# Attention on one Trainium2 core: rings of three single PSUM banks for the two kinds of score tiles

## The reference

```python
B, S, E, H = (8, 256, 256, 16)          # run with x of 8 x 512 x 256, so s = 512
q = split_heads(x @ Wq); k = split_heads(x @ Wk); v = split_heads(x @ Wv)
attn = softmax(einsum('bhqd,bhkd->bhqk', q, k) * e ** (-0.5))
attn = attn + bias[None]                # relative bias, added after the softmax
out = einsum('bhqk,bhkd->bhqd', attn, v)
out = (out - mu) / sqrt(var + EPS) * gamma + beta
x = layernorm(x + out)                  # then: router logits of the next layer = x @ router_w
```

## Time and profile before

| | us |
|---|---|
| runs of the kernel before | 1999.19, 1995.83, 1998.24 (median 1998.24) |
| the profiled execution | 1997.37 |
| its span, first to last instruction | 1995.7 |
| TensorE busy, of the span | 1659.3 |
| VectorE busy | 1182.0 |
| ACT busy | 1081.9 |
| GpSimd busy | 614.4 |
| mean granted clock of TensorE | 0.909 |

### The profile page before, as it was taken

How to read it: one execution, slowest core, us unless ns; L and a number is a source line. 1 busy time by engine, 2 the same in 40 slices (tenths; PEclk the granted TensorE clock), 3 DMA queues, 4 the chain that set the end, 5 groups by cost and what they waited for, 6 DMA issues and landing times. The chain is left out here.

```text
span 1995.7 us, 33219 instructions
## 1 busy us (share of the span) xinstructions
PE 1659.3 (83%) x9891; PEld 1119.0 (56%) x9892; DVE 1182.0 (59%) x1954; ACT 1081.9 (54%) x2276; POOL 614.4 (31%) x560
## 2 busy tenths in 40 slices
PE   4988988662299969899999999935799999999990
PEld 1333333252299836444444444432799999999990
DVE  6999998487611155358999999468233333333324
ACT  6777777450033324127888888724355555555554
POOL 0000000000156422211222222110577777777750
PEclk9999999866599979998999999975899999999995
DMA  5000000035022096703333333067344444444427
GB/s 174 1 0 0 0 0 0 5 104 190 18 65 63 31 316 225 152 1 76 77 97 97 98 97 108 23 215 254 96 68 73 69 69 72 66 64 72 67 23 253
DMA packets 145737, 173.69 MB, mean 87 GB/s; under 512 B 29139, under 2 KB 110430, under 8 KB 145504
## 3 DMA queue, kind: packets, MB, share of 16 engines
q1 hardware_dynamic: 104160, 128.29, 21.0%
q0 software_dynamic: 33248, 43.71, 12.5%
q10 hardware_dynamic: 8224, 0.39, 0.2%
HBM read 111.50 MB, written 66.19 MB: 89 GB/s over the span
## 5 line engine op out<-in xcount | busy, mean ns | idle before, releaser
L1310 PEld LDWEIGHTS f_ht_ps<-f_XT,f_WS 128*128 128x128 f32 x2912 | 358.1, 195 | 15.6 <-DVE f_WS L1403 2.6
L1310 PE MATMUL f_ht_ps<-f_XT,f_WS 128*128 128x128 f32 x2912 | 361.6, 278 | 3.0 <-ACT f_XT L1351 3.0
L1318 PE MATMUL f_y_ps<-W,f_HT 128*128 x1456 | 344.1, 379 | 0.0
L2126 DVE TENSOR_REDUCE att_MX<-att_s_ps 128x2 f32<-128x1024 f32 x256 | 304.7, 1215 | 57.6 <-PE att_s_ps L1886 57.5
L1276 POOL DMA_INDIRECT moe<-f_Y,TOK x182 | 278.2, 1529 | 183.0 <-ACT f_Y L1376 108.9
L2091 ACT ACTIVATE att_PT<-att_st_ps 128x512 f32<-128x512 f32 x512 | 278.6, 595 | 53.7 <-PE att_st_ps L1911 46.1
L1318 PEld LDWEIGHTS f_y_ps<-W,f_HT 128*128 128x128 f32 x1456 | 262.7, 190 | 28.3
L1403 DVE COPY f_WS<-W 128x1024 f32 x182 | 135.2, 743 | 205.0 <-PE f_ht_ps L1310 129.6
L1267 POOL DMA_INDIRECT XG<-x,TOK x182 | 192.0, 1055 | 195.9 <-issue 125.8
L297 PE MATMUL rec_gate<-rec_XC,rec_W 128*128 128x512 f32 x384 | 188.2, 643 | 68.7 <-ACT rec_R L199 42.8
L1411 DVE TENSOR_TENSOR f_Y<-f_y_ps,f_B 128x256 f32<-128x256 f32 x143 | 60.7, 424 | 294.9 <-PE f_y_ps L1318 294.9
(11 more groups left out here) (271 smaller groups left out, 2193.6 us busy)
## 6 DMA issues: line engine op xcount, KB each, us to landing
W<-in_w SPq DMA_DIRECT2D x48, 512.0 KB, 10.0
att_Q<-qk_pairs SPq DMA_DIRECT2D x192, 64.0 KB, 2.8
att_K<-qk_pairs SPq DMA_DIRECT2D x192, 64.0 KB, 3.0
qk_pairs<-prj_HI SPq DMA_DIRECT2D x16, 512.0 KB, 3.8
qk_pairs<-prj_LO SPq DMA_DIRECT2D x16, 512.0 KB, 5.1
hidden<-in_xT SPq DMA_DIRECT2D x8, 512.0 KB, 7.7
x<-n_Y SPq DMA_DIRECT2D x8, 512.0 KB, 3.0
prj_X<-x SPq DMA_DIRECT2D x8, 512.0 KB, 8.9
```

What stands on the lines that cost most here:

```text
L1310: mm = nc.tensor.matmul(ht_ps[r % 2][:, f * P:(f + 1) * P], WS[r % 2][:, at:at + P], XT[r % 2][:, c], start=(c == 0), stop=(c == DC - 1))
L1318: mm = nc.tensor.matmul(y_ps[r % 2][:], HT[r % 2][:, f], W2[:, bass.ds(e * W_EXPERT + f * D, D)], start=(f == 0), stop=(f == FC - 1))
L2126: nc.vector.tensor_reduce(MX[n % 2][:, qc, :, p], s_ps[m % 2][:], AX.X, ALU.max).then_inc(s_mx, 1)
```

## The change

The six banks of the two kinds of scores are divided three and three, each ring of single banks. `scores` numbers its products by half slots and waits for the maximum three back; it raises `s_smm` for both halves. `maximum` takes each bank by itself in two reductions. `scores_T` takes the bank of its number modulo three in place of that of its half, and waits for the exponential three back in place of two. In the router phase `z_ps` is banks 0 and 1 of the score ring and `L_ps` is bank 2 alone, so `logit_products` of a batch waits for the copy of the batch before it. The relative bias still uses `st_ps[0]` and `st_ps[1]` only.

```diff
--- before.py
+++ after.py
@@ -1699,8 +1699,8 @@
         zmv = st.sb("zmv", [P, B, KC, 2])
         zrstd = st.sb("zrstd", [P, B, KC, 1])
         zshift = st.sb("zshift", [P, B, KC, 1])
-        s_ps = [st.ps(f"s_ps{k}", (P, 2, BANK)) for k in range(2)]
-        st_ps = [st.ps(f"st_ps{k}") for k in range(2)]
+        s_ps = [st.ps(f"s_ps{k}") for k in range(3)]
+        st_ps = [st.ps(f"st_ps{k}") for k in range(3)]
         o_ps = st.ps("o_ps")
         x_ps = st.ps("x_ps")
 
@@ -1750,8 +1750,8 @@
         s_st = st.sem("z_stored")
         block = ctx.enter_context(nc.Block())
         LOADS = 12 * 16
-        z_ps = [s_ps[0][:, c] for c in range(DC)]
-        L_ps = [s_ps[1][:, k] for k in range(2)]
+        z_ps = [s_ps[c][:] for c in range(DC)]
+        L_ps = s_ps[2][:]
 
         def rows_of(b):
             return OUT[:, KC * b:KC * (b + 1)]
@@ -1876,17 +1876,14 @@
             def scores(i, qc, half):
                 n, p = i // 2, i % 2
                 k = n % STACKS
-                m = i * KC + qc
-                if half == 1:
-                    if p == 0 and qc == 0:
-                        pe.wait_ge(s_ld[k], LOADS * (n // STACKS + 1))
-                    if m >= 2:
-                        pe.wait_ge(s_mx, m - 1)
+                m = 2 * (i * KC + qc) + 1 - half
+                if half == 1 and p == 0 and qc == 0:
+                    pe.wait_ge(s_ld[k], LOADS * (n // STACKS + 1))
+                if m >= 3:
+                    pe.wait_ge(s_mx, m - 2)
                 at = slice(half * HALF, half * HALF + ROW_M)
-                mm = nc.tensor.matmul(s_ps[m % 2][:, half], Q[k][at, p, qc * P:(qc + 1) * P], K[k][at, p],
-                                      start=True, stop=True)
-                if half == 0:
-                    mm.then_inc(s_smm, 1)
+                nc.tensor.matmul(s_ps[m % 3][:], Q[k][at, p, qc * P:(qc + 1) * P], K[k][at, p],
+                                 start=True, stop=True).then_inc(s_smm, 1)
 
             def maxima(n):
                 pe.wait_ge(s_ms, n + 1)
@@ -1905,10 +1902,10 @@
                 if p == 0 and kc == 0 and half == 0:
                     pe.wait_ge(s_mr[k], 32 * (n // STACKS + 1))
                 m = 2 * (i * KC + kc) + half
-                if m >= 2:
-                    pe.wait_ge(s_p, m - 1)
+                if m >= 3:
+                    pe.wait_ge(s_p, m - 2)
                 at = slice(half * HALF, half * HALF + ROW_M + 2)
-                nc.tensor.matmul(st_ps[half][:], K[k][at, p, kc * P:(kc + 1) * P], Q[k][at, p],
+                nc.tensor.matmul(st_ps[m % 3][:], K[k][at, p, kc * P:(kc + 1) * P], Q[k][at, p],
                                  start=True, stop=True).then_inc(s_stm, 1)
 
             def sums(n, piece):
@@ -1956,7 +1953,7 @@
             def z_transposes(b):
                 pe.wait_ge(s_z, KC * (b + 1))
                 if b == 0:
-                    pe.wait_ge(s_mx, TWO * KC)
+                    pe.wait_ge(s_mx, 2 * TWO * KC)
                     pe.wait_ge(s_w, 32)
                 for c in range(DC):
                     if b >= 1:
@@ -1967,11 +1964,11 @@
 
             def logit_products(b):
                 pe.wait_ge(s_zc, DC * (b + 1))
-                if b >= 2:
-                    pe.wait_ge(s_lc, b - 1)
+                if b >= 1:
+                    pe.wait_ge(s_lc, b)
                 for j in range(KC):
                     for c in range(DC):
-                        mm = nc.tensor.matmul(L_ps[b % 2][:, j * P:(j + 1) * P], ZT[b % 2][c][:, j * P:(j + 1) * P], WG[:, c],
+                        mm = nc.tensor.matmul(L_ps[:, j * P:(j + 1) * P], ZT[b % 2][c][:, j * P:(j + 1) * P], WG[:, c],
                                               start=(c == 0), stop=(c == DC - 1))
                 mm.then_inc(s_lg, 1)
 
@@ -2087,8 +2084,9 @@
                     copy_sums(n - 2)
                 for kc in range(KC):
                     for half in range(2):
-                        act.wait_ge(s_stm, 2 * (i * KC + kc) + half + 1)
-                        nc.scalar.activation(PT[n % 2][:, 2 * half + p, kc], st_ps[half][:], ACT.Exp, scale=SCALE).then_inc(s_p, 1)
+                        m = 2 * (i * KC + kc) + half
+                        act.wait_ge(s_stm, m + 1)
+                        nc.scalar.activation(PT[n % 2][:, 2 * half + p, kc], st_ps[m % 3][:], ACT.Exp, scale=SCALE).then_inc(s_p, 1)
                     if p == 0 and kc == 1 and n + 1 < NGROUPS:
                         copy_maxima(n + 1)
                     for b, s in join_slots(i * KC + kc):
@@ -2121,12 +2119,13 @@
                 n, p = i // 2, i % 2
                 if p == 0 and qc == 0 and n >= 2:
                     dve.wait_ge(s_ms, n - 1)
-                m = i * KC + qc
-                dve.wait_ge(s_smm, m + 1)
-                nc.vector.tensor_reduce(MX[n % 2][:, qc, :, p], s_ps[m % 2][:], AX.X, ALU.max).then_inc(s_mx, 1)
+                for half in (1, 0):
+                    m = 2 * (i * KC + qc) + 1 - half
+                    dve.wait_ge(s_smm, m + 1)
+                    nc.vector.tensor_reduce(MX[n % 2][:, qc, half, p:p + 1], s_ps[m % 3][:], AX.X, ALU.max).then_inc(s_mx, 1)
 
             def split(n):
-                dve.wait_ge(s_mx, 2 * KC * (n + 1))
+                dve.wait_ge(s_mx, 4 * KC * (n + 1))
                 if n >= 2:
                     dve.wait_ge(s_mt, n - 1)
                 own.after(nc.vector.tensor_copy(MS[n % 2][:, :, :, 0], MX[n % 2][:]))
@@ -2181,7 +2180,7 @@
             def copy_logits(b):
                 dve.wait_ge(s_lg, b + 1)
                 nc.vector.tensor_copy(logits[:, KC * b:KC * (b + 1)],
-                                      L_ps[b % 2].rearrange("p (j e) -> p j e", j=KC)[:, :, 0:E]).then_inc(s_lc, 1)
+                                      L_ps.rearrange("p (j e) -> p j e", j=KC)[:, :, 0:E]).then_inc(s_lc, 1)
 
             def join_step(b, s):
                 if s < KC:
```

## The result

The changed kernel takes 2021.98 us (median of 4 runs, 2019.5 to 2022.45), the kernel before in the same comparison 1997.9. The ratio is 1.0120, 95% interval 1.0104 to 1.0136: +24.1 us. Forecast were 2012 us and a range of 1998 to 2026.

The account below looks back on a forecast made before the run. VectorE was taken to bound the loop, with TensorE and ACT close. Loop +11, lead-in +2.8, last slots -1.5 and tail +3.3 gave +15.6 on 1997.37; plus 0.9 for the median, less 2, 2012 us, range 1998 to 2026.

Parts of the forecast that it names:

- the four signs: Attention's stages: loop +11 us, lead-in +2.8, last 16 slots -1.5, tail +3.3.
- the signs named: Observations that would confirm the forecast, among them 512-column reductions near 0.68 us and steady batches of 50 to 51.5 us.
- Maxima over one bank: Loop, VectorE: each added reduction costs 0.07 us, 2.0 us a batch, bounds 0.9 and 4.6.
- The ring of scores: Loop: three single banks leave 1.8 us of work in reserve; VectorE starves at four transposes, 1.0 us a batch.
- The ring of transposed scores: Loop: waiting three exponentials back removes TensorE's 0.43 us wait for ACT and VectorE's 0.49 us wait.
- Lead-in: Before the loop: four heads' fourth score waits for the first maximum, 0.7 us each, +2.8 us, bounds 0 and 4.
- Tail: After attention's slots: one router bank makes products wait for the previous batch's copy, +3.3 us, bounds 2 and 5.
- Last slots: Last 16 slots, without scores: one more transposed product in reserve covers ACT waits, -1.5 us, bounds -3 and 0.
- rival of full fixed cost: Loop: each added reduction costs 0.16 us, loop +27, total 2030; chance 0.10.
- that of absorbed starvation: Loop: the rings absorb VectorE's 2.97 us of waits a batch; total 1995, or 1987 with cheap reductions; chance 0.16.
- The stall moves: Loop: VectorE's 2.05 us a batch behind GpSimd vanishes (1998) or a second appears (2028); chance 0.06, half each.
- It does not do what it says: Loop: the transposed-score ring's gain shows nowhere; starvation stays 2.97, batch 51.4, loop +15, total 2018; no separate chance.

Follow-up runs that it names:

- e_s4: Kernel before with only the maxima split into one-bank reductions: four single score banks, two for transposed scores, two router banks; 2000.5 us, ratio 1.0017.
- b_pool: Kernel before with GpSimd's residual of a batch put ahead of its group addition; 1989.5 us, ratio 0.9965.
- e_st2: Changed kernel with the transposed scores back at two banks, one bank left unused; 2031.0 us, ratio 1.0167.
- e_pool: Changed kernel with GpSimd's residual of a batch put ahead of its group addition; 1997.8 us, ratio 1.0001.
- e_tail: Changed kernel with a second router bank in the tail, taken from the transposed scores; 2017.2 us, ratio 1.0098.
- e_fill2: e_st2 plus two unread products into its free bank, once a batch, ahead of a second score in TensorE's queue; 2026.4 us, ratio 1.0126.

## Why the prediction was right, and where it was not

The direction, the range and the four signs were right; the size was low by 10 us (+14 forecast, +24 measured). The mechanism was right in part, and what it left out is the largest single item: TensorE's stop at VectorE's stall and the half clock behind it. The upper edge of the range came from the price of a reduction, so that 2022 lies inside it is partly luck. Of the signs named, a batch of 50 to 51.5 us came true for the plain batch alone; the mean of the five is 53.0. By its steps:

- **Maxima over one bank.** The added time of an instruction was sized well: 0.60 us of pitch against 0.595 foreseen (1.12 / 2 + 0.035), a lone one 0.68. It was charged at 2.0 us a batch and came through as 0.3 (e_s4), since waits of VectorE paid for it. The text had let the waits shrink by 1.5 us in all, a part of it for this, but had then added 1.0 for the shallower ring. In e_s4, where the ring is as deep as before, they shrank by 1.5 (3.0 to 1.4).
- **The ring of scores.** The forecast compared a reserve of 1.8 us with TensorE's absences, and gave the shallower ring 1.0 us a batch. Where the clock holds this was near the truth: the plain batch has 2.3 us of waits for the 2.5 foreseen, and takes 50.5 us for 50.9. But the forecast never set VectorE's own absence against the ring. The row of that absence stood in the text, as cover for 0.2 us of reductions and as a rival that it might move. This is the step that failed. With TensorE two slots ahead the stall cost 0.94 us a batch (b_pool); with one and a half it costs 1.7, and TensorE itself stops for 1.73 us, and the half clock follows in four places of six. Depth and stall act together: one bank fewer costs 24.4 us with the stall (e_s4 to e_st2, its half clock included), and with the stall gone the loop of the kernel with three and three banks is within 1 us of the other two. The stall also stands six times in the loop, where the rival that moves it counted 7.5.
- **The clock.** No step had it. The clock before was 1.00 in the steady loop, and the text took that as given. Plain batches of the changed kernel are 50.5, below the 50.9 foreseen; the four slow ones add 2.9 + 3.7 + 2.8 + 2.9 = 12.4 us (53.5, 54.2, 53.3, 53.5 less 50.5), which is the miss of the loop and more. In e_st2 the same surplus went to zero when TensorE was kept busy. There a half clock of 3.4 us goes with 1.2 us and one of 6.8 with 2.3; in the changed kernel 6.8 us go with 2.8 to 2.9 and 10.2 with 3.7. That these are all clock was not tested by filling the wait in the changed kernel itself, but the parts add up: six stalls of 1.7 us and 12.4 us are 22.6, and e_pool's loop is 22.9 shorter. The sixth stall has no half clock behind it, and its batch is 53.3 us against 51.6 in e_pool, again 1.7. So against the kernel before, of the loop's 17.7 us 12.4 are the half clock, 4.6 the stall that costs 1.7 in place of 0.94 six times over, and 0.5 the layout itself (363.9 for 363.4 without the stall).
- **The ring of transposed scores.** Right in kind: TensorE's wait for ACT there is gone from its matmuls (2.6 us between 960 and 1260 before, 0.0 after). It was worth 9 us of loop in a kernel that the stall holds up, and 1.2 us a batch where the clock holds, where the forecast had it at the 0.49 of one wait and a part of others.
- **Lead-in.** Mis-sized: 1.04 us a head, not 0.7. The fourth score starts 1.28 us after the first in place of 0.35, since it waits for the first reduction, and then runs by itself. Timeline of TensorE, one such head:

```profile
844.22 0.73 PE L1885 MATMUL att_s_ps<-att_K,att_Q 48*128 48x512 f32 x3
...
845.50 0.49 PE L1885 MATMUL att_s_ps<-att_K,att_Q 48*128 48x512 f32 x1 [0.55 <-DVE att_MX L2125]
...
845.92 0.66 PE L1950 MATMUL att_o_ps<-ident,att_O 128*128 128x128 f32 x4
```

- **Tail.** Mechanism right to the row, and its size too: the single bank costs 3.3 us (35.1 less e_tail's 31.8). The 3.3 became 4.9 because the 16 instructions ran at the lower clock (1.3 of the 1.6), which they do with two router banks as well. Copies 2 and 3 stand 3.75 us apart for the two foreseen.
- **Last slots.** -2.8 for -1.5, by the same mechanism.

The rival of full fixed cost (2030) is refuted by e_s4 (loop +2.2 where it had +27), that of absorbed starvation (1995) by the waits in the loop. "The stall moves" was refuted too: it stayed where it was, and still decided. "It does not do what it says" is refuted by e_st2: the third bank of the transposed scores shows. As for the rule of the Trainium skill that was weighed (VectorE: DVE Perf Modes, "The TRN2 errata"), the estimate from its fixed 120 cycles would have put 0.125 us on each added reduction; the trace has 0.06 to 0.09 for a slot's second one (1.20 a slot in place of 1.11 to 1.14), and what reached the time was 0.01. On the missed step, the rows show a TensorE that idled for 1.73 us and was then granted half its clock, in four places of six. The Trainium skill (TensorE: Matmul & The Clock Gate, Part 1) says that the lower rate is the default which activity releases, and that the watching runs on its own and not from the kernel's start; the two places of six without a drop would fit the second half, though no run here tests it.

## What to carry to other kernels

A ring is sized against the longest stop on either side, not against the mean load: look for single instructions with outlying durations (here 2.2 us for 16 columns) and ask how far the other engine gets meanwhile. Where that engine is TensorE, add what the clock takes when it stops, as a second cost that the trace of a well-fed kernel cannot show. And look for the cause of the stall first: moving one GpSimd operation ahead of another (b_pool) was worth 7 us in the kernel before and 24 in the changed one, and gave a kernel that is faster than both.

## What the runs showed that was not expected

- Splitting a reduction of two PSUM banks into two of one cost 0.3 us a batch of 32 slots (e_s4): the reductions took 1.9 us more a batch and the waits for scores 1.5 less. That the waits shrink because VectorE can start on the first half earlier is the likely reason, not a tested one.
- Two products without use, 2 us of TensorE's time, shortened the batches with a drop by 1.2 to 2.3 us (e_fill2).
- The same wait of 1.73 us is followed by the half clock or not: four of six in the changed kernel, four of six in e_st2. What decides between them is open.
- A split of 16 columns on VectorE that meets a GpSimd addition of 1024 columns a partition stands until that addition ends (1151.01 + 2.18 = 1153.19 in the changed kernel; GpSimd's operation ends at 1150.80 + 2.35 = 1153.15). In e_pool it met a shorter one and lost 0.27 us. The reductions from PSUM that ran beside the addition ahead of it (1148.28 + 2.38 us, `L1855`) were not slowed: 0.60 us of pitch there too.
